# Sorting edges into cells: one-hot rows built column by column, weights turned first, smaller first batches

## The chip, the cores and the metric

One core of a Trainium2 chip runs the whole program. The metric is the device time of one execution in microseconds (us). The engines are TensorE (PE in the profile, its weight loads PEld), VectorE (DVE), ScalarE (ACT), GpSimd (POOL), and SyncE (SP), which only issues transfers and waits.

## The reference

Four graph layers follow each other on 1250 nodes with 512 features and 21250 edges (10000 pairs in both directions and a self loop for each node; `dst` is sorted in the input, but not cell by cell). Each layer normalises `x`, applies ReLU and adds its result to `x`.

- Layer 0: `x @ W_self.T + mean over neighbours(x) @ W_neigh.T + bias`, layer norm.
- Layer 1: two weighted graph convolutions with degree scaling, then a row norm.
- Layer 2: a message per edge from `h[src]` and 128 edge features through two linear layers, a sum per destination, a GRU cell, a batch norm with given statistics.
- Layer 3: a weighted neighbour sum and a linear layer.

Layers 0, 1 and 3 need `segment_sum` over the edges with three weightings: 1, `edge_weight`, `edge_weight1`. Layer 2 folds `W2` and `W_ih` into one matrix per gate (the products `m` and `c` below), which depends on weights only.

## The kernel before, in words

**Cells.** The 1250 nodes make NT = 10 tiles of 128. An edge belongs to one of 10 x 10 = 100 cells (tile of `dst`, tile of `src`). The kernel sorts the edges by cell into rows of the DRAM tensor `cell_rows`, each cell padded to whole chunks of 128, and later turns each chunk into a 128 x 128 block of three adjacency matrices by one product on PE.

**Where an edge goes.** Edges lie as 128 partitions x 168 columns (J = 168; only 167 are used, columns are grouped in 34 spans of SPAN = 5). DVE makes the one-hot rows `oh1` (columns x B1 = 101 cells, bf16) in four wide comparisons (L1506). PE counts with two products per span (`count_span`, L1146): `before` is the count of each cell in earlier spans of all partitions, row by row, and `total` the count over all. DVE turns these into `base_b`, the first place of each span in each cell, split into a high and a low byte (L1522 to L1539). PE then gives in `rank_spans` (L1155, L1158) for a slot of up to 5 spans the place of the first edge of a kind, from `sums1` (the sum of the five one-hots of a span, by DVE's `sum_spans`) and `row_of` (a selector of rows, L1509). DVE's `pick_spans` (L1560, L1568) multiplies that with the one-hots and sums; with `own`, the number of equal cells earlier in the same span (L1572 to L1575), this is the place of each edge. Seven short steps (L1583 to L1589) make the row index `idx1` of a batch of spans (`BATCHES` = 0, 2, 6, 14, 24, 34 in spans; `SUMMED` gives the slots) and release POOL by `order_ready[0]`.

**The cell scatter.** POOL waits for a batch, copies payload and indices of a span into one of two rings (`index_span`, L712 and L713), and issues one indirect DMA of 128 rows for each column (`scatter_span`, L720): 168 in all. When all have landed, SP loads `cell_rows` back (`cells_loaded`), and ACT, DVE, POOL and PE start to build blocks (L875, L1742, L772, L1213).

**What runs beside the scatter.** PE turns ten weight blocks (`turn_weights`, transposes, L1133), ACT copies them out of PSUM (L833) into one of two buffers `ws`, and SP loads raw weights (two buffers, L515) and stores the turned ones. For the three `ih` blocks PE also makes the products `m` and `c` (L1191) right behind each block. DVE sorts the edges once more by the tile of `dst` (`places`, with the product `prefix2` on PE), then SP loads `x`, and DVE, PE and ACT do the first normalisation and two linear products for each of ten tiles (`he`, `hsT`, `ys`, `zs`; PE L1123). SP also zeroes the DRAM tensors `cell_rows` (one transfer) and `dst_rows` (six of 2 MB), both ahead of the first raw weight in its queue.

**Order.** Each engine runs its own list in order; semaphores tie them. On PE the list was: counts of all spans, wait for `base_ready`, then slots and weight blocks in turn.

Of the kernel before, what the change touches and what calls it, by code (L numbers as in the profile page):

```python
# [29 lines left out]
BF16 = mybir.dt.bfloat16  # L30
# [4 lines left out]
P = 128  # L35
# [11 lines left out]
J = -(-(JV + 1) // COL) * COL  # L47
# [37 lines left out]
def build_gnn(nc, x_in, src_in, dst_in, attr_in, w_in, w1_in, w_self, w_neigh, b0, gamma0, beta0,  # L85
# [19 lines left out]
    with ExitStack() as ctx:  # L105
# [92 lines left out]
        ones_b = sort_part(P // 2, BF16)  # L198
        base_b = sort_part(B1 // 2 + 1, BF16)[:, 0:B1]
# [3 lines left out]
        assert scur[0] <= 2 * AW  # L203
# [14 lines left out]
        cell_b = temp(SPAN * SPANS // 2).bitcast(BF16)  # L218
        own, same = temp(SPAN * SPANS), temp(SPAN * SPANS)
# [101 lines left out]
        ering = sb("ering", [P, COL, EW])  # L321

# [14 lines left out]
        sums1_ready = sem("sums1_ready")  # L337
        weights_copied = sem("weights_copied")
# [71 lines left out]
        PREFIX2_AFTER = 7  # L410
        X_AFTER = 8
# [4 lines left out]
        for n, (name, third) in enumerate(blocks):  # L416
            act_jobs += [("w", n, k) for k in range(5 if n == 0 else KT)]
            if blocks[n - 1][0][0:2] == "ih":
                act_jobs += [("m", blocks[n - 1][1], k) for k in range(KT)] + [("c", blocks[n - 1][1])]
# [35 lines left out]
        wj = {b: A[("w", b, KT - 1 if b else 4)] + 1 for b in range(len(blocks))}  # L455
        raw_src = {"w1h": w1_2, "ih0": w_ih, "ih1": w_ih, "ih2": w_ih, "hh0": w_hh, "hh1": w_hh,
# [24 lines left out]
        def _(sp):  # L481
# [11 lines left out]
            sp.wait_ge(zero_ready, 1)  # L493
            zc = (CELL_CHUNKS + SPARE) * 4
            sp.dma_start(cell_rows.rearrange("(p c) w -> p (c w)", p=P), h.rearrange("p t d -> p (t d)")[:, 0:zc]).then_inc(cells_zeroed, 16)
            for k in range(KT):
                sp.dma_start(b2_col[:, k:k + 1], b2_2[k * P:(k + 1) * P].rearrange("(p a) -> p a", a=1)).then_inc(b2_loaded, 16)
            zd = (DST_CHUNKS + SPARE) * EW
            part = zd // 6
            dz = dst_rows.rearrange("(p c) w -> p (c w)", p=P)  # L500
            for k in range(6):
                sp.dma_start(dz[:, k * part:(k + 1) * part], h.rearrange("p t d -> p (t d)")[:, 0:part]).then_inc(zeroed, 16)

            for n, (name, third) in enumerate(blocks):
                if n == X_AFTER:
                    sp.wait_ge(sorted_all, 1)
                    sp.wait_ge(x_free, 1)
                    for t in range(NT):
                        m = P if t + 1 < NT else LAST
                        sp.dma_start(xs[0:m, t], x_in[t * P:t * P + m, :]).then_inc(xe_loaded[t], 16)  # L510
# [6 lines left out]
                if n == 3:  # L517
                    sp.wait_ge(zeroed, 16 * 6)
# [3 lines left out]
                if n == len(blocks) - 1:  # L522
                    sp.wait_ge(b2_ready, 1)
                    for k, v in enumerate((b0, gamma0, beta0)):
                        sp.dma_start(vec[:, k], v.rearrange("(a f) -> a f", a=1).to_broadcast([P, D])).then_inc(vec_loaded, 16)
                if blocks[n - 2][0][0:2] == "ih":
                    gate = blocks[n - 2][1]
                    sp.wait_ge(act_read, A[("c", gate)] + 1)
                    sp.dma_start(wt_dram[f"m{gate}"], m_out.rearrange("p k f -> p (k f)")).then_inc(m_stored, 16)
                    sp.dma_start(c_dram[gate], c_out).then_inc(m_stored, 16)  # L530
# [10 lines left out]
            sp.wait_ge(c_scattered[1], 16 * (J - SPAN * (SPANS // 2)))  # L541
# [3 lines left out]
            edge_v = attr_in[0:JV * P, :].rearrange("(p j) f -> p j f", j=JV)  # L545
            for q in range(2):
                sp.dma_start(ering[:, 4 * q:4 * q + 4, 0:DE], edge_v[:, 4 * q:4 * q + 4, :]).then_inc(e_loaded[q], 16)
# [124 lines left out]
        def _(pool):  # L672
# [23 lines left out]
            nc.gpsimd.memset(own, 0.0)  # L696
            nc.gpsimd.memset(base_b, 0.0)
            nc.gpsimd.memset(cell_b[:, J:], 0.0)
            nc.gpsimd.memset(oh1[:, J:].rearrange("p j b -> p (j b)"), 0.0).then_inc(const_ready, 1)
            nc.gpsimd.memset(ones[:], 1.0).then_inc(const_ready, 1)  # L700

            pool.wait_ge(cells_zeroed, 16)
# [22 lines left out]
            rest = J - SPAN * (SPANS - 1)  # L725
            for n in range(len(BATCHES) - 1):
# [15 lines left out]
            pool.wait_ge(zeroed, 16 * 6)  # L742
# [86 lines left out]
        def _(act):  # L829
# [9 lines left out]

            act.wait_ge(edges_loaded, 16 * 4)  # L840
# [3 lines left out]
            for n in range(len(blocks)):  # L844
                m = n - 2
                if 0 <= m < len(stored_blocks):
                    act.wait_ge(wt_stored[m % 2], 16 * (m // 2 + 1) + (16 if m % 2 == 0 else 0))
                elif m >= 0:
                    act.wait_ge(for_act, A[("c", blocks[m][1])] + 1)
                if blocks[n][0] == "self":  # L850
                    root(("he", 1), one_rstd[:])
                for k in range(KT):
                    copy_job(("w", n, k), ws[:, n % 2, k])
                if n == 0:
                    copy_job(("w", 0, 4), tiles[:, 0])
                if blocks[n][0] == "neigh":
                    root(("he", 0), one_rstd[:])
                if blocks[n - 1][0][0:2] == "ih":
                    gate = blocks[n - 1][1]
                    if gate:  # L860
                        act.wait_ge(m_stored, 32 * gate)
                    for k in range(KT):
                        copy_job(("m", gate, k), m_out[:, k])
                    copy_job(("c", gate), c_out)
# [231 lines left out]
        def _(pe):  # L1096
# [45 lines left out]
            def count_span(g):  # L1142

                n = columns(g) * B1
                for job, left in (("before", later[:, SPANS - 1 - g:SPANS - 1 - g + P]), ("total", ones_b)):
                    ins = nc.tensor.matmul(dve_bank(job)[:, 0:n], left, hot_span(g, columns(g)), start=g == 0, stop=g == SPANS - 1)  # L1146
                    if g == SPANS - 1:
                        ins.then_inc(for_dve, 1)
# [12 lines left out]

            pe.wait_ge(sort_const, 1)
# [4 lines left out]
            pe.wait_ge(const_ready, 8)  # L1167
            pe.wait_ge(base_ready, 1)
            for n in range(len(blocks)):
                if n < 2:  # L1170
                    rank_spans(n)
                elif n == 2:
                    rank_spans(2)
                    rank_spans(3)
                elif n < 5:
                    rank_spans(n + 1)
                turn_weights(n)
                if n == 6:
                    rank_spans(6)
                if blocks[n - 1][0][0:2] == "ih":  # L1180

                    gate = blocks[n - 1][1]
# [898 lines left out]
```

## Time and profile before

| | us |
|---|---|
| median of 3 runs (lowest 1367.62, highest 1372.83) | 1371.41 |
| the profiled execution | 1371.79 |
| its span in the trace | 1370.0 |
| first indirect DMA of the cell scatter starts | 43.85 |
| last one starts | 290.04 |
| cells are back, first GpSimd product of the block stage starts | 296.82 |

Shares of the span by engine: PE busy 87%, DVE 74%, POOL 51%, ACT 42%. These are averages over stages. From 44 to 296 us PE is busy 161.68 of 252 us, DVE 142.21 and POOL 179.85; from 296 us to the end PE is busy 1013.42 of 1074. So the first 296 us have to be read by their own waits. A DMA_INDIRECT row on POOL is the time in which GpSimd writes one indirect transfer. In a timeline the first column is the start, the second the duration, and the brackets give the idle time before and what ended it. Instructions of one engine overlap a little in such rows, so the cost of one in a run of many is the distance between starts, not the duration.

### The profile page before, as it was taken

The page shows a single profiled execution, that of the slowest core. Times are in us where ns is not written, and L with a number is a line of the kernel's source. Part 1 is how long each engine was busy: PE and PEld are TensorE (multiplying, and loading weights), DVE is VectorE, ACT ScalarE, POOL GpSimd, SP SyncE. Part 2 cuts the span into 40 slices and gives each one's busy share as a digit, 9 for nine tenths or more (in the row PEclk, how much of TensorE's full clock was granted, in tenths as well). Part 3 has the DMA queues.
Part 4 walks back from the last instruction along what each step waited for, and adds up shares of the span by engine and source line. Part 5 has one row for each costly group of instructions (what it writes and reads, how often), then busy time and mean ns, then how long its engine had stood idle before and what let it go on. Part 6 is the DMA issues. An engine that isn't in the chain of part 4 may idle for free.

```text
span 1370.0 us, 20255 instructions
## 1 busy us (share of the span) xinstructions
PE 1192.8 (87%) x4298; PEld 745.9 (54%) x4298; DVE 1016.8 (74%) x2113; ACT 572.2 (42%) x1461; POOL 700.4 (51%) x828
## 2 busy tenths in 40 slices
PE   5468499429999999999998899999999899998998
PEld 2343244214444445558876555454454588886787
DVE  9796845129999998642387688898888899888433
ACT  0221121027777730220011388787788833334211
POOL 0577777768888843776676366666666100000000
PEclk9679699859999999999999999999999999999999
DMA  8851512130000036333226677776777200002231
GB/s 331 313 197 40 199 63 79 55 113 18 27 20 25 12 146 223 112 114 131 82 88 181 204 224 221 223 234 207 226 213 221 58 1 0 1 0 89 77 96 37
DMA packets 87258, 167.89 MB, mean 123 GB/s; under 512 B 16124, under 2 KB 44670, under 8 KB 84644
## 3 DMA queue, kind: packets, MB, share of 16 engines
q1 hardware_dynamic: 59588, 102.69, 22.5%
q0 software_dynamic: 25472, 59.97, 14.4%
q10 hardware_dynamic: 2144, 4.59, 1.0%
q8 instruction: 25, 0.41, 0.1%
q14 instruction: 29, 0.24, 0.1%
HBM read 115.96 MB, written 51.23 MB: 122 GB/s over the span
## 4 chain that ended last, share of the span: by engine, by line
PE 62%; POOL 14%; issue 10%; DVE 8%; DVEq 2%; DMA 2%; ACT 1%; POOLq 0%; SPq 0%; ACTq 0%
PE pb L1348 11%; POOL cell_rows L720 10%; PE pb L1248 6%; PE pb L1240 6%; PE pb L1443 5%; PE pb L1213 5%; PE pb L1416 4%; PE pb L1418 4%; PE pb L1417 4%; PE pb L1362 3%; PE pb L1364 2%; PE pb L1365 2%; PE pb L1123 2%; PE pb L1341 2%; DMA p_rows<-tiles 2%
## 5 line engine op out<-in xcount | busy, mean ns | idle before, releaser
L765 POOL DMA_INDIRECT dst_rows<-ering,gidx x168 | 171.7, 1022 | 101.3 <-issue 95.4
L1348 PE MATMUL pb<-arena 128*128 128x512 f32 x368 | 191.2, 602 | 14.1 <-ACT arena L990 13.8
L720 POOL DMA_INDIRECT cell_rows<-tiles,gidx x168 | 166.8, 993 | 68.1 <-issue 47.4
L819 POOL DMA_INDIRECT arena<-p_rows,arena x96 | 100.5, 1047 | 78.6 <-issue 24.9
L1213 PE MATMUL pb<-arena 128*128 128x384 f32 x268 | 96.7, 504 | 42.4 <-POOL arena L772 42.2
L875 ACT ACTIVATE arena<-iota,free 128x128 f32<-128x128 f32 x266 | 92.3, 394 | 85.9 <-DMA free<-cell_rows 39.2
L1917 DVE TENSOR_TENSOR arena<-pb,arena 128x512 f32<-128x512 f32 x184 | 122.3, 683 | 5.7 <-DMA arena<-p_rows,arena 3.3
L1924 DVE SCALAR_TENSOR_TENSOR low<-arena,high 128x512 fp32r<-128x512 f32 x138 | 95.2, 690 | 31.4 <-ACT high L997 22.0
L819 POOL DMA_INDIRECT arena<-p_rows,ws x88 | 89.1, 1013 | 53.9 <-issue 29.0
L1213 PE MATMUL pb<-tiles,arena 128*128 128x384 f32 x264 | 94.4, 501 | 15.2 <-DVE arena L1761 9.4
L1759 DVE TENSOR_TENSOR arena<-pb,arena 128x192 f32 x266 | 94.1, 354 | 12.8 <-PE pb L1213 12.7
L1364 PE MATMUL pb<-high,low 128*128 128x512 f32 x138 | 99.5, 721 | 2.5 <-DVE arena L1932 2.0
L1213 PEld LDWEIGHTS pb<-arena 128*128 128x128 f32 x268 | 48.8, 193 | 85.2 <-ACT arena L880 43.4
L1417 PE MATMUL pb<-gru_low,high 128*128 128x512 f32 x240 | 93.5, 390 | 0.0
L1761 DVE TENSOR_TENSOR arena<-pb,arena 128x192 f32 x266 | 92.6, 348 | 0.1
L1123 PE MATMUL pb<-ws,tiles 128*128 128x512 f32 x200 | 89.2, 593 | 2.8 <-issue 1.6
L1240 PE MATMUL pb<-arena 128*128 128x256 f32 x400 | 88.2, 380 | 2.0 <-DVE arena L1856 1.4
L997 ACT ACTIVATE high<-arena 128x512 fp32r<-128x512 f32 x138 | 84.9, 615 | 7.2 <-DVE arena L1917 5.8
L1240 PEld LDWEIGHTS pb<-arena 128*128 128x128 f32 x400 | 75.8, 190 | 16.0 <-issue 4.3
L1213 PEld LDWEIGHTS pb<-tiles,arena 128*128 128x128 f32 x264 | 45.5, 189 | 63.9 <-ACT arena L880 34.0
L1348 PEld LDWEIGHTS pb<-arena 128*128 128x128 f32 x368 | 55.7, 191 | 45.0 <-ACT arena L990 19.7
L1443 PE MATMUL pb<-parts 128*128 128x512 f32 x300 | 74.1, 407 | 5.9 <-DVE parts L1980 4.2
(331 smaller groups left out, 2550.6 us busy)
## 6 DMA issues: line engine op xcount, KB each, us to landing
dst_rows<-arena SPq DMA_DIRECT2D x6, 2046.0 KB, 17.5
ering<-in_edge_attr_dram SPq DMA_DIRECT2D x41, 256.0 KB
arena<-adj SPq DMA_DIRECT2D x10, 640.0 KB, 4.1
arena<-dst_rows SPq DMA_DIRECT2D x24, 264.0 KB
arena<-wt_gru SPq DMA_DIRECT2D x48, 128.0 KB
ws<-dst_rows SPq DMA_DIRECT2D x22, 264.0 KB
arena<-in_x_dram SPq DMA_DIRECT2D x18, 256.0 KB, 7.8
arena<-in_L_gnn_W_hh_dram SPq DMA_DIRECT2D x3, 1024.0 KB
```

Of the source, the lines that this page charges most:

```text
L720: nc.gpsimd.indirect_dma_start(cell_rows[:, :], bass.IndirectOffsetOnAxis(gidx[:, SPAN * a + k:SPAN * a + k + 1], 0), cring[:, a, k], None ...
L765: nc.gpsimd.indirect_dma_start(dst_rows[:, :], bass.IndirectOffsetOnAxis(gidx[:, k:k + 1], 0), ering[:, k, :], None).then_inc(e_scattered[ ...
L819: nc.gpsimd.indirect_dma_start(rows[:, k % GROUP, :], None, p_rows[:, :], bass.IndirectOffsetOnAxis(edge_rows(k).bitcast(I32)[:, 0, DE:DE ...
L1123: ins = nc.tensor.matmul(b[:, 0:wide], x[:, k], w[:, k], start=m == 0, stop=m == n - 1)
L1213: nc.tensor.matmul(pb[k % 4][:, 0:3 * P], ohs[:, k], ohd(k, 1).rearrange("p a m d -> p (a m d)"), start=True, stop=True).then_inc(block_do ...
L1240: ins = nc.tensor.matmul(b[:, 0:wide], blocks_of[:, s], rows_of[:, s, 0:wide], start=s == 0, stop=s == NT - 1)
L1348: nc.tensor.matmul(e_bank(k)[:], erowT[:, k % 4], w1e_sb, start=True, stop=True).then_inc(edge_mm, 1)
L1364: nc.tensor.matmul(sums, hot, high[:, k % 4], start=k % 2 == 0, stop=False)
L1417: nc.tensor.matmul(bank[:], parts[0][:, k], low_w, start=False, stop=False)
L1443: ins = nc.tensor.matmul(b[:], a3[:, t % 2, left, k], h3[:, right, k], start=first and k == rows_of[0] and left + right == 0, stop=last an ...
L1917: vtt(row, e_bank(k)[:], row, ALU.add).then_inc(msg_added, 1)
L1924: vstt(low_part[:, k % 4], rows[:, k % GROUP], 0.0, high[:, k % 4].bitcast(F32), ALU.max, ALU.subtract).then_inc(msg_ready, 1)
```

## The change

- **One-hots per column.** `oh1` is made by 168 `tensor_scalar` instructions of 102 bf16 elements, each comparing a row of cell numbers with a per-partition scalar in SBUF (a pointer operand: `cell_f[:, j:j+1]`, now fp32). B1 is 102. There are five parts for PE (`O_PARTS`) instead of four.
- **One count product per span.** `total` is no longer counted by 34 products; DVE reduces `before`, and one fp32 product with `last_row` (a matrix whose row 127 is ones) copies its last row, where all counts stand, to every partition.
- **Moved off DVE.** `row_of` is made by ACT with two activations (Abs, then Relu of 1 minus it) over 128 x 4352; `own` is made by POOL (four subtractions, three additions) and ACT (Abs, Relu over 128 x 680). DVE's long zeroing of `h` is gone; one memset of the edge ring (128 x 1056) is the source of zeros.
- **Weights first.** The first raw weights are at the head of SP's queue after the edge columns; PE turns block 0 ahead of the counts. `cell_rows` is zeroed by two transfers behind the second raw weight, `dst_rows` by 24 smaller transfers behind the tenth. Turned `ih` blocks go to a place of their own (`ih_turned`), and all fifteen products `m` and `c` follow after the tenth block, with the last slot and `prefix2` between them. Loading `x` comes after their stores in SP's queue.
- **Small batches.** `BATCHES` = 0, 1, 2, 4, 8, 14, 24, 34 and ten slots instead of eight; the scatter leaves out the unused column 168, so it issues 167.

```diff
-        B1 = CELLS + 1
+        B1 = CELLS + 2
-        O_PARTS = [0, 9, 18, 27, SPANS]
-        BATCHES = [0, 2, 6, 14, 24, SPANS]
-        SUMMED = [0, 2, 6, 10, 14, 19, 24, 29, SPANS]
+        O_PARTS = [0, 9, 18, 26, 31, SPANS]
+        BATCHES = [0, 1, 2, 4, 8, 14, 24, SPANS]
+        SUMMED = [0, 1, 2, 4, 8, 11, 14, 19, 24, 29, SPANS]
...
+                if n == 1:
+                    sp.wait_ge(zero_ready, 1)
...
+                    for k in range(CELL_ZEROS):
+                        sp.dma_start(cz[:, k * cell_zeros:(k + 1) * cell_zeros], zeros[:, 0:cell_zeros]).then_inc(cells_zeroed, 16)
...
+            for k in range(DST_ZEROS):
+                sp.dma_start(dz[:, k * dst_zeros:(k + 1) * dst_zeros], zeros[:, 0:dst_zeros]).then_inc(zeroed, 16)
...
+            for gate in range(3):
+                sp.wait_ge(act_read, A[("c", gate)] + 1)
+                sp.dma_start(wt_dram[f"m{gate}"], m_out.rearrange("p k f -> p (k f)")).then_inc(m_stored, 16)
+                sp.dma_start(c_dram[gate], c_out).then_inc(m_stored, 16)
+            sp.wait_ge(sorted_all, 1)
+            sp.wait_ge(x_free, 1)
...
+            for d in range(1, SPAN):
+                nc.gpsimd.tensor_tensor(apart[:, d - 1, :, d:], cell5[:, :, d:], cell5[:, :, 0:SPAN - d],
+                                        ALU.subtract).then_inc(own_apart, 1)
...
-            rest = J - SPAN * (SPANS - 1)
+            rest = USED - SPAN * (SPANS - 1)
...
+            nc.scalar.activation(row_of, iob_f[:, 0:SPANS].unsqueeze(2).to_broadcast([P, SPANS, P]), ACT.Abs,
+                                 bias=row_p).then_inc(row_ready, 1)
...
-                for job, left in (("before", later[:, SPANS - 1 - g:SPANS - 1 - g + P]), ("total", ones_b)):
-                    ins = nc.tensor.matmul(dve_bank(job)[:, 0:n], left, hot_span(g, columns(g)), start=g == 0, stop=g == SPANS - 1)
...
+                ins = nc.tensor.matmul(dve_bank("before")[:, 0:n], later[:, SPANS - 1 - g:SPANS - 1 - g + P],
+                                       hot_span(g, columns(g)), start=g == 0, stop=g == SPANS - 1)
...
+            pe.wait_ge(const_ready, 9)
+            turn_weights(0)
             pe.wait_ge(sort_const, 1)
...
+            pe.wait_ge(counts_summed, 1)
+            nc.tensor.matmul(dve_bank("total")[:, 0:B1], last_row, before, start=True, stop=True).then_inc(for_dve, 1)
+            pe.wait_ge(base_ready, 2)
+            pe.wait_ge(row_ready, 2)
+            rank_spans(0)
+            turn_weights(1)
+            rank_spans(1)
...
-                vtt(oh1[:, c], iob[:, 0:B1].unsqueeze(1).to_broadcast([P, n, B1]),
-                    cell_b[:, c].unsqueeze(2).to_broadcast([P, n, B1]), ALU.is_equal).then_inc(hot1_ready, 1)
-
-            vts(row_of, iob_f[:, 0:SPANS].unsqueeze(2).to_broadcast([P, SPANS, P]), row_p, None, ALU.is_equal)
...
+                for j in range(SPAN * O_PARTS[q], min(SPAN * O_PARTS[q + 1], J)):
+                    ins = vts(oh1[:, j], iob[:, 0:B1], cell_f[:, j:j + 1], None, ALU.is_equal)
+                ins.then_inc(hot1_ready, 1)
...
+            sum_spans(0)
...
+            nc.vector.tensor_reduce(before, whole(dve_bank("before")), AX_X, ALU.add).then_inc(dve_read, 1)
+            dve.wait_ge(dve_read, V["before"] + 1)
+            dve.sem_inc(counts_summed, 1)
...
+            vts(cnti, dve_bank("total")[:, 0:B1], float(P - 1), None, ALU.add).then_inc(dve_read, 1)
...
             nc.vector.memset(xs[:, NT - 1], 0.0).then_inc(x_free, 1)
+            dve.wait_ge(for_act, A[("c", 2)] + 1)
```

## Rows read from the trace of the kernel before

**Rows 1.** The page: the chain that ended last, shares by line.
```profile
PE pb L1348 11%; POOL cell_rows L720 10%; PE pb L1248 6%; PE pb L1240 6%; PE pb L1443 5%; PE pb L1213 5%; PE pb L1416 4%; PE pb L1418 4%; PE pb L1417 4%; PE pb L1362 3%; PE pb L1364 2%; PE pb L1365 2%; PE pb L1123 2%; PE pb L1341 2%; DMA p_rows<-tiles 2%
```

**Rows 2.** The chain in order of time, first 297 us: start, duration, piece.
```profile
13.41 17.08 PE pb L1146 x67
43.85 1.34 POOL cell_rows L720
...
290.04 2.10 DMA cell_rows<-tiles,gidx
296.82 1.05 POOL arena L772
```

**Rows 3.** Timeline of POOL: the first scatters of two spans that follow each other.
```profile
66.47 0.98 POOL L720 DMA_INDIRECT cell_rows<-tiles,gidx  x1 [0.79 <-issue]
...
73.68 0.99 POOL L720 DMA_INDIRECT cell_rows<-tiles,gidx  x1 [0.81 <-issue]
```

**Rows 4.** Timeline of DVE from the cell numbers to the first indices.
```profile
7.02 0.24 DVE L1497 TENSOR_SCALAR arena<-arena 128x168 int32<-128x168 int32 x1
7.18 0.24 DVE L1498 TENSOR_SCALAR arena<-arena 128x168 int32<-128x168 int32 x1
...
8.37 18.04 DVE L1506 TENSOR_TENSOR arena<-arena 128x4545 bf16<-128x4545 bf16 x4
26.32 2.48 DVE L1509 TENSOR_SCALAR arena<-arena 128x4352 bf16<-128x4352 f32 x1
...
30.59 0.68 DVE L1522 TENSOR_REDUCE arena<-pb 128x101 f32<-128x505 f32 x1 [0.37 <-PE pb L1146]
...
31.90 0.21 DVE L1526 TENSOR_SCALAR arena<-arena 128x101 f32<-128x101 f32 x1
...
34.64 0.21 DVE L1538 CAST arena<-arena 34x101 bf16<-34x101 int32 x1
...
37.92 0.68 DVE L1560 TENSOR_TENSOR arena<-pb,arena 128x505 f32<-128x505 f32 x1
...
40.78 0.17 DVE L1583 TENSOR_TENSOR arena<-arena 128x10 int32<-128x10 f32 x1
...
42.02 0.17 DVE L1589 CAST idx<-arena 128x10 int32<-128x10 f32 x1
```

**Rows 5.** DVE instructions with a pointer operand: timeline, then one line's durations.
```profile
6.35 0.15 DVE L1490 CAST arena<-arena 128x104 bf16<-128x104 f32 x1
6.42 0.27 DVE L1491 TENSOR_SCALAR arena<-arena 128x128 bf16<-128x128 f32 x1
6.61 0.24 DVE L1492 TENSOR_SCALAR arena<-arena 128x162 bf16<-128x162 f32 x1
```
```profile
L1641 DVE SCALAR_TENSOR_TENSOR arena<-arena x11: 380/383/404, 133.1 to 136.2; 128x168 f32<-128x168 bf16 x11
```

**Rows 6.** Timelines of PE's weight loads and of PE, first 60 us.
```profile
18.43 0.15 PEld L1146 LDWEIGHTS pb<-arena 128*128 128x128 bf16 x1 [0.27 <-issue]
```
```profile
36.29 0.38 PE L1158 MATMUL pb<-arena 128*128 128x101 bf16 x2
45.22 4.47 PE L1133 MATMUL pb<-ident,arena 128*128 128x128 f32 x20 [8.55 <-DMA arena<-in_L_gnn_W_dram]
```

**Rows 7.** Windows: busy us (instructions) of each engine, TensorE clock, DMA share, GB/s.
```profile
0.00:25.00 25.00, 11.59 (x42) 4.78 (x43) 22.86 (x18) 2.08 (x3) 3.08 (x21) 1.00 0.74 294
```

**Rows 8.** Groups of ACT instructions by line and shape.
```profile
L1042 ACT CAST parts<-arena 128x1280 fp32r<-128x1280 f32 x10 | 12.6, 1262 | 5.1 <-PE pb L1443 5.1
```

**Rows 9.** Timeline of PE: products of one gate, last linear products before the cells.
```profile
112.85 17.33 PE L1191 MATMUL pb<-ws,arena 128*128 128x512 f32 x40
...
241.85 13.90 PE L1123 MATMUL pb<-ws,tiles 128*128 128x512 f32 x32
```

**Rows 10.** Timelines of SP (loading x) and DVE (first tile half normalised).
```profile
143.42 4.87 SPq L510 DMA_DIRECT2D arena<-in_x_dram  x10
```
```profile
168.47 0.50 DVE L1699 TENSOR_SCALAR arena<-arena 128x512 f32<-128x512 f32 x1
```

More of the change, by code:

```diff
@@ L46 @@
 COL = 8
-J = -(-(JV + 1) // COL) * COL
+USED = JV + 1
+J = -(-USED // COL) * COL
 PAIR = 2 * P
@@ L217, in build_gnn @@
         st_f, dt_f = temp(J), temp(J)
-        cell_b = temp(SPAN * SPANS // 2).bitcast(BF16)
-        own, same = temp(SPAN * SPANS), temp(SPAN * SPANS)
+        cell_f = temp(SPAN * SPANS)
+        own, own_rest = temp(SPAN * SPANS), temp(SPAN * SPANS)
+        apart = temp(4 * SPAN * SPANS).rearrange("p (d g j) -> p d g j", d=4, g=SPANS)
+        last_row = temp(P)
         row_p = temp(1)
@@ L844, in _ @@
             for n in range(len(blocks)):
-                m = n - 2
-                if 0 <= m < len(stored_blocks):
+                m = {2: 0, 3: 1, 4: 2, 8: 4, 9: 3}.get(n)
+                if m is not None:
                     act.wait_ge(wt_stored[m % 2], 16 * (m // 2 + 1) + (16 if m % 2 == 0 else 0))
[L848 to L851, printed above, removed]
                 for k in range(KT):
-                    copy_job(("w", n, k), ws[:, n % 2, k])
+                    copy_job(("w", n, k), turned_block(n)[:, k])
                 if n == 0:
                     copy_job(("w", 0, 4), tiles[:, 0])
[L856 to L864, printed above, removed]
+            for gate in range(3):
+                if gate:
+                    act.wait_ge(m_stored, 32 * gate)
+                for k in range(KT):
+                    copy_job(("m", gate, k), m_out[:, k])
+                copy_job(("c", gate), c_out)
+            root(("he", 0), one_rstd[:])
+            root(("he", 1), one_rstd[:])
             def flat(t4):
@@ L1166, in _ @@
                     count_span(g)
[L1167 to L1182, printed above, removed]
-                    pe.wait_ge(w2_loaded, 16)
-                    pe.wait_ge(b2_ready, 1)
-                    pe.wait_ge(act_read, wj[n - 1])
-                    for k in range(KT + 1):
-                        job = ("m", gate, k) if k < KT else ("c", gate)
-                        b = to_act(job)
-                        for o in range(KT):
-                            left = w2_raw[:, o, k * P:(k + 1) * P] if k < KT else b2_wide[:, o]
-                            ins = nc.tensor.matmul(b[:], left, ws[:, (n - 1) % 2, o], start=o == 0, stop=o == KT - 1)
-                        ins.then_inc(for_act, 1)
-                if n == 6:
-                    rank_spans(7)
-                if n == PREFIX2_AFTER:
-                    pe.wait_ge(totals_ready, 1)
-                    sort_products("prefix2", B2)
@@ new lines, in _, with fold @@
+            turn_weights(5)
+            rank_spans(6)
+            turn_weights(6)
+            turn_weights(7)
+            rank_spans(7)
+            turn_weights(8)
+            rank_spans(8)
+            turn_weights(9)
+            def fold(gate, products):
+                for k in products:
+                    job = ("m", gate, k) if k < KT else ("c", gate)
+                    b = to_act(job)
+                    for o in range(KT):
+                        left = w2_raw[:, o, k * P:(k + 1) * P] if k < KT else b2_wide[:, o]
+                        ins = nc.tensor.matmul(b[:], left, ih_turned[:, gate, o], start=o == 0, stop=o == KT - 1)
+                    ins.then_inc(for_act, 1)
@@ L1199, in _ @@
+            pe.wait_ge(w2_loaded, 16)
+            pe.wait_ge(b2_ready, 1)
+            pe.wait_ge(act_read, wj[7])
+            fold(0, range(0, 2))
+            rank_spans(9)
+            fold(0, range(2, 5))
+            fold(1, range(KT + 1))
+            fold(2, range(0, 2))
+            pe.wait_ge(totals_ready, 1)
+            sort_products("prefix2", B2)
+            fold(2, range(2, KT + 1))
             pe.wait_ge(sorted_all, 1)
```

190 lines of the change are left out of this document (102 added, 88 removed).

## The prediction

> **What bounds the kernel now.** I read the page's chain first. Most of it is PE after 296 us, but one item is not PE: the cell scatter on POOL holds 10% of the chain [rows 1]. The chain in order of time shows why [rows 2]: up to 30.5 us it is the counts on PE, which follow DVE's one-hots, then nothing long but scatters from 43.85 to 290.04 us, the landing, the load of the cells, and the first product of the block stage at 296.82. Only then does the rest of the kernel begin, and the diff leaves that rest alone. So the change can move the time in two ways only: by when the first scatter starts, and by how long the row of scatters takes. Everything else it moves lies beside the scatter and counts only if it ends later than the cells.
>
> The POOL timeline gives the pace: a span of five takes 73.68 - 66.47 = 7.21 us [rows 3]. The batches after the first hardly ever make it wait. The profiled execution took 1371.79 us, of which the span is 1370.0; the median of the runs is 1371.41, 0.4 less, and I take that 0.4 off at the end.
>
> **The path to the first scatter now** [rows 4]. Cell numbers from 7.02; one-hots from 8.37 to 26.41; row selector and small steps to 30.2; counts reduced from 30.59; base places 31.90 to about 35.1; span sums and own ranks until 37.92; two picks until 40.78; seven index steps until 42.19; 1.66 us later the scatter at 43.85 [rows 2]. Now the same path with the change, step by step.
>
> *Start.* DVE no longer clears h (3.4 us) ahead of the cell numbers, so the edge columns decide. They cannot be there before about 3.2 us (their issue) and were there at 7.02. I take 4.6. The numbers took 8.37 - 7.02 = 1.35 us and get one more semaphore: one-hots from 6.0 (bounds 4.7 to 8.4).
>
> *One-hots per column.* This is the price that decides. Two neighbours without a pointer operand, 168 elements, start 0.16 us apart [rows 4]. With reductions at 0.68 us for 505 elements and 0.17 for ten, an element costs about 1.03 ns, and a single-input step half of it: 0.16 is 0.087 of elements and 0.07 fixed. With a pointer operand the trace has two cases [rows 5]. The eleven of L1641 start 3.1/10 = 0.31 us apart (on finer reading 0.304) for 168 elements at 1.03 ns, 0.173: fixed 0.13. L1491 is followed 0.19 us later, with 128 elements at half price, 0.066: fixed 0.124. So a pointer costs some 0.055 us more for each instruction. I take 0.127 fixed and, for 102 narrow elements, 0.027, between nothing and the half price 0.053: 0.154 us a column, bounds 0.13 and 0.18. 168 x 0.154 = 25.9 us against 18.0 now. One-hots end at 31.9, 5.5 us later than now.
>
> The Trainium skill has a rule for this (VectorE: DVE Perf Modes, on the TRN2 errata, where SBUF sources pay a fixed extra latency per instruction): 58 cycles and the elements divided by the perf mode, which it gives as four for bf16 tensor_scalar. By it a column would cost (58 + 102/4)/0.96 = 87 ns, an estimate, and all 168 would take 14.6 us. The same section says that many small tiles pay the fixed cost each time and large ones once, which speaks against this edit. The rows without a pointer are near its 58 cycles; those with one are not.
>
> *Counts.* PE ran them at first one in 0.15 + 0.27 = 0.42 us [rows 6], later half of that. There are 34 now instead of 68, and weight block 0 ahead of them: 20 transposes, 4.47 us [rows 6], from about 12 us when its raw weights land (both loads, 2.3 MB at 294 GB/s [rows 7], take 7.9 us from about 5, the first of them less). Done at 16.5, before DVE is; so DVE bounds, and only the last part of three spans is left: 3 x 0.42 = 1.3. Counts end at 33.2. DVE hides this with the sums of slot 0 and the low bits of the ends.
>
> *Total.* Reduction 0.1 + 0.68; semaphore 0.1; the fp32 product 0.5 (bounds 0.2 and 1: a transpose costs 0.22, an fp32 product with 512 columns 0.43); then the chain from L1526 to L1538, 2.74 us now [rows 4], less two steps of 0.25, 2.25; two copies 0.45. Base places at 37.3. Now they were ready at 35.1.
>
> *First slot.* PE 0.6 (its last products for two spans ended at 36.67 [rows 6], 0.6 after the sums that released them); one pick instead of two, (40.78 - 37.92)/2 = 1.43 us; index steps 42.19 - 40.78 = 1.41; own ranks no longer on this path, saving 2.0 us where they stood. Indices ready at 40.7, first scatter 1.66 us later: **42.4**.
>
> So the wide steps taken off DVE (row selector 2.48 us, one reduction, own ranks, one pick, the clearing) pay for the slower one-hots and leave 43.85 - 42.4 = 1.4 us.
>
> *One scatter fewer.* The last spans keep the same pace as the first, five scatters in a span and 0.8 us between spans, (7.21 - 0.83)/5 = 1.28 us each, so 167 instead of 168 saves 1.28 us.
>
> **What costs nothing, and its cover.** ACT's row selector: 1280 elements take 1.262 us [rows 8], so about 3.9 us for 4352; twice that and the two short ones end near 13 us; it is wanted at 37. POOL's own ranks: seven short operations before 12 us, wanted at 39. The batches: after the first, POOL is busy 7.21 us a span, DVE needs 1.43 for a pick, 1.4 for indices and 1 to 1.4 for sums, so the second batch (5.2 us of DVE work) is in time, and so are the wider ones; on PE each slot stands behind weight blocks that need some 7 us each (two-buffer loading), at most two between slots, against batches of 14 us and more. Zeroing dst_rows (12.6 MB, 37 us of queue) moves from under the first weights to under the scatter, wanted at 290. Own place for the turned ih blocks: nothing.
>
> The longest move is behind it. The three folds (17.3 us each [rows 9]) now stand together after the tenth block, near 96 us; the first store of m waits in SP's queue behind the 12.6 MB of zeros, so ACT's second fold starts near 131, prefix2 near 144 instead of 130, and x is loaded near 157 instead of 143 [rows 10]. The first tile then is normalised near 183 instead of 169, and ten tiles at 7.3 us, PE's work up to the cells, end near 258. Now PE ends at 255.8 [rows 9], since it was held by the last fold until 181. The cells come at 294: a cover of some 35 us.
>
> **Sum.** 1371.8 - 1.4 - 1.3 = 1369.1; less 0.4 for the median: **1368.7 us**, 0.2% faster, which is no difference that can be told. I call that bound 0.5%, 6.9 us, about what this measurement can tell from no change. The likeliest case's own range: column price 0.13 to 0.18 gives -4.0 and +4.4, start and product -1.5 and +2.5: 1363 to 1375.
>
> **Rivals.**
>
> *A. The pointer is hidden, as if it were read under the instruction before.* A column then costs 0.07 + 0.027 = 0.097 us; one-hots end at 6.0 + 16.3 = 22.3 and PE bounds the counts: 16.5 + 13 x 0.42 + 21 x 0.21 = 26.4 (24.5 if the clock is already up after the weights). That is 6.8 us earlier than above; first scatter at 35.6, total 1361.9, faster. For it: L1491 starts only 0.07 us after the instruction before it, which has 104 elements [rows 5], so that both together are no dearer than two without pointer. Against it: the eleven of L1641. The Trainium skill's 87 ns (the section named above) would give the same, since PE bounds. It decides below 0.129 a column, where 1364.5 is reached.
>
> *B. The column instructions do not overlap at all.* A step whose result is awaited costs 0.15 + 0.05 for the pointer + 0.027 = 0.23 us and so would these, for example while POOL's additions and DVE want the same memory path. 168 x 0.23 = 38.6, first scatter 42.4 + 12.7 = 55.1, total 1381.4: slower. For it: 168 distinct outputs in close order are nowhere in the trace. Against: every unlinked pair overlaps by 0.08. It decides from 0.21 a column, where 1378.3 is reached.
>
> *C. The work beside the scatter overtakes it.* If folds, stores and zeros push the load of x past 190 us instead of 157, the ten tiles end after the cells and each further us is lost. At 203 us it costs some 10: 1378.7. For it: three waits in a row on the stores of m. Against: 35 us of cover.
>
> *D. The change does its first step and no more*: the first scatter comes earlier, but POOL then waits for slot 1 behind weight block 1. The order has rank_spans(0), block 1, rank_spans(1): 16 transposes, 3.6 us, against 6.4 us of scatters. Each us above that is lost; it would eat up A's gain only with a late second weight, landed by 15 us. It ends within 0.5%.
>
> **How the numbers follow.** Forecast and D together 0.53; A 0.33; B 0.08; C 0.04; 0.02 for the rest, on the slow side. So faster 0.34 (A and the edge of the forecast), same 0.53, slower 0.13. The range reaches over A's value with its faster clock and over the forecast's upper end: 1360 to 1376; B and C are left out, 0.12, and some edge of A.
>
> **What would show it.** In the profile after: distance of the column one-hots' starts (0.154; 0.10 in A; 0.23 in B); the end of the counts (33.2); the first scatter at 42.4 (A 35.6, B 55); last scatter 2.7 us earlier than 290.04; first block product near 294; no idle time of POOL between batches; PE's last linear product near 258; the stretch behind the cells, 1073.2 us, unchanged. The prediction is wrong if the column price is outside 0.13 to 0.18, or if the later stage changes its length.

## Result: 1.6% slower, and the loss is in a loop that the diff doesn't touch

The changed kernel took 1393.78 us (median of 4 runs, 1390.96 to 1399.89) against 1372.12 us before (4 runs, 1367.62 to 1373.95): ratio 1.0162, interval 1.0133 to 1.0191. The forecast was 1368.7, with a range of 1360 to 1376. The profiled execution took 1390.96 us.

Up to the block stage almost everything came as forecast. DVE's and PE's timelines of the changed kernel, answering to [rows 4, 6]:

```profile
4.44 0.25 DVE L1548 TENSOR_SCALAR arena<-arena 128x168 int32<-128x168 int32 x1 [1.59 <-DMA arena<-in_dst_dram]
...
5.99 27.60 DVE L1557 TENSOR_SCALAR arena<-arena 128x102 bf16<-128x102 bf16 x168 [0.25 <-DVE arena L1552]
...
35.14 0.69 DVE L1583 TENSOR_REDUCE arena<-pb 128x102 f32<-128x510 f32 x1 [0.34 <-PE pb L1185]
...
39.05 0.21 DVE L1600 CAST arena<-arena 34x102 bf16<-34x102 int32 x1
...
42.44 0.17 DVE L1635 CAST idx<-arena 128x5 int32<-128x5 f32 x1
```
```profile
10.96 4.42 PE L1173 MATMUL pb<-ident,arena 128*128 128x128 f32 x20 [10.96 <-DMA arena<-in_L_gnn_W_dram]
...
31.62 3.41 PE L1185 MATMUL pb<-arena 128*128 128x510 bf16 x8 [1.36 <-DVE arena L1557]
```

One-hots start at 5.99 and end at 33.59, counts end at 35.03, base places are there at 39.26. POOL's timeline and PE's around the cells [rows 2, 9] have the rest: first scatter 44.19, and the first block product at 296.49, 1.5 us earlier than the 298.00 of before.

```profile
44.19 1.19 POOL L750 DMA_INDIRECT cell_rows<-tiles,gidx  x1 [0.91 <-POOL gidx L743]
```
```profile
249.19 13.90 PE L1163 MATMUL pb<-ws,tiles 128*128 128x512 f32 x32
296.49 4.18 PE L1268 MATMUL pb<-arena 128*128 128x384 f32 x6 [33.40 <-POOL arena L807]
```

So the change stood 1.5 us ahead when the "unchanged" rest began. The windows of each kernel cut that rest in two: the block stage (first block product to the first product of the next stage), and all behind it. First before, then after; the columns are the engines' busy time, PE's granted clock, DMA share and GB/s.

```profile
296.80:500.00 203.20, 185.77 (x532) 94.39 (x532) 190.28 (x661) 146.20 (x396) 172.19 (x181) 0.99 0.09 31
500.00:1370.00 870.00, 827.65 (x3160) 554.36 (x3160) 643.29 (x1110) 377.54 (x972) 344.61 (x387) 0.99 0.43 134
```
```profile
295.30:521.90 226.60, 193.73 (x532) 102.01 (x532) 191.35 (x659) 146.24 (x396) 171.92 (x181) 0.93 0.09 29
521.90:1389.00 867.10, 825.33 (x3160) 552.78 (x3160) 642.83 (x1112) 377.30 (x972) 347.67 (x387) 0.99 0.43 134
```

The same 532 products take 24 us more: from product to product (298.00 to 500.54 us before, 296.49 to 523.12 after) the stage is 226.6 us long instead of 202.5 (+24.1). Behind it the kernel is 3.6 us shorter. Together: -1.5 + 24.1 - 3.6 = +19.0, the difference of the two spans.

Who waits in the block stage? The view of DVE's waits has a row in the changed kernel that the kernel before doesn't have: the front addition of the block loop (L1804; L1759 before) stands idle 18 times, 25.6 us in all, and nothing that the profile shows ends the wait.

```profile
DVE arena L1804 <- issue: 25.6, 18, 4.0
```

Its timeline puts the long ones 28 us apart, six of them, 3.68 to 4.02 us each. 28 us is one pass of DVE's block loop (32 chunks), and between two of them, in mid pass, stands a short one of 0.3 us:

```profile
351.51 0.36 DVE L1804 TENSOR_TENSOR arena<-pb,arena 128x192 f32 x1 [4.02 <-issue]
...
363.86 0.36 DVE L1804 TENSOR_TENSOR arena<-pb,arena 128x192 f32 x1 [0.29 <-issue]
...
379.44 0.36 DVE L1804 TENSOR_TENSOR arena<-pb,arena 128x192 f32 x1 [3.84 <-issue]
```

In the kernel before, the same place of the loop has 1.11 us (`PE pb L1213` ended it), and the middle none:

```profile
349.43 0.36 DVE L1759 TENSOR_TENSOR arena<-pb,arena 128x192 f32 x1 [1.11 <-PE pb L1213]
```

What arrives in these stretches is code. The DMA view has queue q14, kind "instruction", 8 KB a packet. In the window 330 to 500 us of the kernel before it moved 5 packets, in 330 to 523 us of the changed kernel 34. Before, then after:

```profile
q14 instruction: 5, 0.04, 0.1%
```
```profile
q14 instruction: 34, 0.28, 0.6%
```

**The theory.** DVE's program comes in pieces of 8 KB, which is 128 instructions of 64 bytes in the compiled program. The block loop has 284 instructions. The change puts 176 more instructions on DVE ahead of it (168 columns for 4 wide comparisons are nearly all of it), so the loop's first instruction moves from number 670 to 846, counted in the compiled programs. 284 instructions lie in three pieces or in four, by where the first of them stands. In four, each return to the loop's head finds its code gone, and it is read again: 37 pieces in the whole stage, against 7 before. **The rival**: the added work itself (DVE's instructions, the zeroing of dst_rows now under the scatter, POOL's or SP's new order) disturbs the stage.

The Trainium skill (Runtime: NRT & Kernel Launch, Instruction fetch mechanics) has the rule in general: a taken branch whose target isn't in the window of two blocks of 16 KiB stalls until it is fetched. That rule spoke against this change, and the prediction didn't weigh it. The packets here are of 8 KB, not 16, and two blocks of 256 instructions would hold this loop at number 846 as well as at 670, so by its sizes this change should have cost nothing here. The Trainium skill's total of 32 KiB would fit: it is four packets, three of the loop and one read ahead. That is an argument, and no row shows it. The runs below test the place.

### The profile page after: what moved, and what is told of

Read it like the earlier page. It is cut to its first block, busy times and chain, and to the rows that moved or that the text cites. A ratio compares the mean times of both kernels' runs of the same rounds, so it can differ in the third digit from the quotient of the medians.

```text
span 1389.0 us, 20391 instructions
## 1 busy us (share of the span) xinstructions
PE 1200.4 (86%) x4268; PEld 752.3 (54%) x4268; DVE 1022.2 (74%) x2286; ACT 580.9 (42%) x1465; POOL 704.9 (51%) x836
## 4 chain that ended last, share of the span: by engine, by line
PE 44%; POOL 19%; issue 18%; DVE 8%; DMA 6%; DVEq 3%; SPq 1%; POOLq 1%; ACT 1%; ACTq 0%
PE pb L1403 11%; POOL cell_rows L750 9%; POOL dst_rows L800 6%; PE pb L1498 5%; PE pb L1471 4%; PE pb L1268 4%; PE pb L1473 4%; PE pb L1472 4%; PE pb L1417 3%; PE pb L1419 2%; PE pb L1420 2%; DVE arena L1557 2%; PE pb L1396 2%; DVE arena L1806 2%; DMA ering<-in_edge_attr_dram 1%
## 5 line engine op out<-in xcount | busy, mean ns | idle before, releaser
L1268 PE MATMUL pb<-tiles,arena 128*128 128x384 f32 x264 | 104.4, 542 | 31.5 <-DVE arena L1806 28.2
L1804 DVE TENSOR_TENSOR arena<-pb,arena 128x192 f32 x266 | 94.0, 353 | 34.7 <-issue 25.6
L1268 PEld LDWEIGHTS pb<-tiles,arena 128*128 128x128 f32 x264 | 52.0, 208 | 82.3 <-issue 33.9
L1268 PEld LDWEIGHTS pb<-arena 128*128 128x128 f32 x268 | 50.1, 195 | 74.5 <-ACT arena L920 34.9
L872 ACT ACTIVATE one_rstd<-one_rstd 128x1 f32<-128x1 f32 x50 | 10.1, 203 | 182.7 <-DVE one_rstd L1720 98.9
L1295 PEld LDWEIGHTS pb<-arena 128*128 128x128 f32 x400 | 75.8, 190 | 16.0 <-issue 5.3
L807 POOL TENSOR_TENSOR tiles<-tiles,free 128x512 f32<-128x512 f32 x66 | 68.0, 1050 | 26.2 <-DVE tiles L1787 25.4
```

The source lines that it names most:

```text
L1268: nc.tensor.matmul(pb[k % 4][:, 0:3 * P], ohs[:, k], ohd(k, 1).rearrange("p a m d -> p (a m d)"), start=True, stop=True).then_inc(block_do ...
L1295: ins = nc.tensor.matmul(b[:, 0:wide], blocks_of[:, s], rows_of[:, s, 0:wide], start=s == 0, stop=s == NT - 1)
L1804: vtt(front, sums[:, :, 0:HALF], front, ALU.add).then_inc(front_added, 1)
```

## The experiments

They ran on two other chips, each ratio against runs of the kernel before on the same chip: runs 1, 2, 3 (48 added) and 6 where it took 1355.11 us, the others where it took 1354.53. (The difference to 1372 lies behind the block stage: 850 us there for 869.) The totals expected of runs 1, 2, 3 and 6 were worked out from the first chip's 1372 us, so their differences and stages are to be compared, not the totals. None of them leaves out or changes what is computed; the eighth adds work whose results nobody reads.

**1 and 2. The changed kernel, its loop moved by 8 and by 32 instructions.** The added instructions do nothing but count on a semaphore of their own.

```diff
             link(nc.vector.tensor_copy(counting, iota1[:]))
+            for _ in range(8):        # 32 in the second
+                dve.sem_inc(pad, 1)
```

> The changed kernel with 8 more DVE instructions (semaphore increments that nothing waits for) in DVE's idle time, just ahead of the block loop. Theory 1 (code loading): DVE's block loop has 284 instructions; the profile after shows five 8 KB code loads (128 instructions each) in every turn, where the kernel before shows none once the loop runs. Its last instructions have slid into a fourth such piece, and with the next piece that is loaded ahead, five do not stay resident. 8 more keep it there: stall of about 4 us at each of the loop's returns, block stage near 227 us, total 1391 to 1396. Theory 2 (the table loads at the head of each turn, or traffic, have become slower, not the place of the code): also 1391 to 1396. A control: the padding alone costs nothing.

> The same with 32 instead of 8, which pushes the start of the loop over a 128-instruction border, so that it lies in three pieces. Theory 1: no stall at the returns, block stage 203 us, total 1391 - 24 = 1367 (1364 to 1371), about the kernel before less the 1.6 us that its first products come earlier. Theory 2: no difference from 8, 1391 to 1396.

8 more: ratio 1.0173 (1.0131 to 1.0214), stage 227.3 us, six long idle times of 3.5 to 3.7 us. 32 more: **0.9961 (0.9948 to 0.9974)**, stage 202.25 us. The DMA view again, 8 more (330 to 523 us), then 32 more (330 to 495 us), and of the latter the window of the stage:

```profile
q14 instruction: 34, 0.28, 0.5%
```
```profile
q14 instruction: 4, 0.03, 0.1%
```
```profile
295.07:497.32 202.25, 185.22 (x532) 94.55 (x532) 191.03 (x662) 145.08 (x393) 170.91 (x180) 0.99 0.09 29
```

All of the change's work is in this kernel, and the loss is gone. The rival falls.

**3 and 4. The kernel before, its loop moved by 48 and by 80.** Number 718 stands as 846 does to a border (both 78 past a multiple of 128), 750 as 878.

```diff
             link(nc.vector.tensor_copy(counting, iota1[:]))
+            for _ in range(48):       # 80 in the other
+                dve.sem_inc(pad, 1)
```

> The kernel before, with nothing of the change, and 48 such instructions ahead of the loop, so that it starts at the same place within 128 as in the changed kernel (it adds 176, which is 128 + 48). Theory 1: the stall appears, total 1372 + 24 = 1396 (1392 to 1400). Theory 2: 1372, since nothing of the change is in it.

> The kernel before with 80 empty DVE instructions (semaphore increments) just ahead of its block loop, where 48 cost 1.8%. Code loading by position: the loop begins at DVE instruction 750, and with the code ahead of it its 284 instructions lie in four pieces of 128, at most, with none read again; no row of four idle microseconds at the loop's returns, some 6 fetches in the block stage, stage 202.5 us, ratio 0.998 to 1.002. Rival, that instructions ahead of the loop cost by their number or by the time they take: 80 should cost more than 48 did, ratio 1.02 or above.

48 more: **1.018 (1.0155 to 1.0204)**, stage 227.4 us, 37 pieces of code read in it, six long idle times of 3.7 to 3.9 us. 80 more: 1.0001 (0.9985 to 1.0017), stage 202.3 us, 6 pieces. Nothing but empty instructions makes the old kernel as slow as the new one, and more of them make it fast again. The waits of DVE with 48:

```profile
DVE arena L1760 <- issue: 26.1, 19, 3.9
```

**5. The changed kernel with a shorter loop.**

```diff
-PLACED = 4 * TURN
+PLACED = 2 * TURN
```

> The changed kernel with 16 chunks in each pass of DVE's block loop in place of 32: the loop is 142 instructions long and is run through twice as often. Code loading: a loop of that length is never longer than three pieces, so no return stalls, the stage takes about 203 us and the ratio is that of the changed kernel with 32 empty instructions, 0.996 (0.993 to 0.999). Rival, that the stall belongs to the return itself (a register, the table load): twice as many returns, twice as many stalls, some 45 us, ratio 1.035.

The loop's start moves as well, to number 714, which is 74 past a border.

1.0002 (0.9989 to 1.0016). No long idle time and 5 pieces of code in the stage, as the theory says; but the time missed its range. The stage took 206.8 us, not 203: every return costs DVE about 0.8 us of idle time, and there are more than twice as many.

```profile
322.99 0.36 DVE L1804 TENSOR_TENSOR arena<-pb,arena 128x192 f32 x1 [0.87 <-PE pb L1268]
```

In the loop of 32 chunks six ordinary returns cost 1.05 to 1.1 us each, put down to PE. I hadn't priced a return.

**6. Wide comparisons in place of the 168 columns.** It tries both halves of the story: fewer instructions ahead of the loop (number 684), and the column's price.

```diff
+        cell_b = temp(SPAN * SPANS // 2).bitcast(BF16)
...
+            link(nc.vector.tensor_copy(cell_b[:, 0:J], cell_f[:, 0:J]))
...
-                for j in range(SPAN * O_PARTS[q], min(SPAN * O_PARTS[q + 1], J)):
-                    ins = vts(oh1[:, j], iob[:, 0:B1], cell_f[:, j:j + 1], None, ALU.is_equal)
-                ins.then_inc(hot1_ready, 1)
+                c = slice(SPAN * O_PARTS[q], min(SPAN * O_PARTS[q + 1], J))
+                n = c.stop - c.start
+                vtt(oh1[:, c], iob[:, 0:B1].unsqueeze(1).to_broadcast([P, n, B1]),
+                    cell_b[:, c].unsqueeze(2).to_broadcast([P, n, B1]), ALU.is_equal).then_inc(hot1_ready, 1)
```

> The changed kernel with the four wide one-hot comparisons of before in place of the 168 column instructions (five parts). One-hots 18 us instead of 27.6, so first scatter near 34.8 instead of 44.2; the loop then starts 162 instructions earlier, in three pieces. Theory 1: 1391 - 24 - 9 = 1358 (1355 to 1363). Theory 2: 1391 - 9 = 1382.

0.9994 (0.9979 to 1.001): no stall (stage 202.6 us), but the first scatter came at 46.56, not 34.8, and later than with the columns (43.91 in the second run, on the same chip). I was wrong on this one. The timeline over all engines shows a chain across four of them:

```profile
5.88 14.89 POOL L724 TENSOR_TENSOR arena<-arena 128x136 f32<-128x136 f32 x4 [0.91 <-DVEq L1554]
6.28 18.89 DVE L1560 TENSOR_TENSOR arena<-arena 128x4590 bf16<-128x4590 bf16 x5
...
20.80 0.77 ACT L881 ACTIVATE arena<-arena 128x680 f32<-128x680 f32 x1 [13.99 <-POOL arena L724]
...
27.27 1.12 PE L1174 MATMUL pb<-ident,arena 128*128 128x128 f32 x4 [12.50 <-ACT ws L869]
...
28.18 9.31 PE L1186 MATMUL pb<-arena 128*128 128x510 bf16 x34
```

POOL's four subtractions for the own ranks, 1.20 us together in the changed kernel, take 14.89 us while DVE's wide comparisons run. One by one, three of the four end just behind a comparison: at 11.43, 16.39 and 20.77 us, where comparisons end at 11.22, 16.23 and 20.65. ACT waits for them, and behind ACT's wait stand its copies of weight block 0 out of PSUM; PE waits for those, and behind PE's wait stand the counts. The columns cost DVE 8.7 us more (27.60 against 18.89) and leave POOL room; the wide form pays it back at another place.

**7. The same, with ACT's order changed**: the copies of block 0 first, then the own ranks' steps and the two copies into pay1. PE's counts no longer stand behind POOL.

```diff
-            act.wait_ge(own_apart, SPAN - 1)
-            apart_flat = apart.rearrange("p d g j -> p (d g j)")
-            nc.scalar.activation(apart_flat, apart_flat, ACT.Abs).then_inc(own_equal, 1)
...
             for n in range(len(blocks)):
...
                 if n == 0:
                     copy_job(("w", 0, 4), tiles[:, 0])
+                    act.wait_ge(own_apart, SPAN - 1)
+                    apart_flat = apart.rearrange("p d g j -> p (d g j)")
+                    nc.scalar.activation(apart_flat, apart_flat, ACT.Abs).then_inc(own_equal, 1)
...
```

> The changed kernel with five wide bf16 comparisons in place of the 168 columns, and on ScalarE the copies of weight block 0 out of PSUM ahead of the own ranks' steps, so that TensorE's counts don't stand behind them. DVE's comparisons end at 25.1 us as in the run without the new order, the counts near 26.5 in place of 37.5, the base places near 31, the first scatter at 35.5 (34.5 to 37), last scatter 8 us earlier than in the changed kernel; DVE's loop begins at instruction 684, so no stall. Time against the kernel before: 9.5 to 12 us less, ratio 0.992 (0.990 to 0.994). Rival, that GpSimd's own ranks, held up by the wide comparisons until 21 us, set the end: own ranks then come after 30 us and the first scatter at 40 or later, ratio 0.996.

**0.9908 (0.9891 to 0.9925), 1343.35 us against 1354.53: faster than both kernels.** DVE's comparisons are as long as in the sixth run, POOL's subtractions too; only who stands behind them changed. PE's timeline and POOL's:

```profile
11.14 4.50 PE L1174 MATMUL pb<-ident,arena 128*128 128x128 f32 x20 [11.14 <-DMA arena<-in_L_gnn_W_dram]
15.44 4.79 PE L1186 MATMUL pb<-arena 128*128 128x510 bf16 x18
...
25.09 0.74 PE L1186 MATMUL pb<-arena 128*128 128x510 bf16 x3 [0.48 <-DVE arena L1560]
```
```profile
35.73 1.19 POOL L751 DMA_INDIRECT cell_rows<-tiles,gidx  x1 [0.91 <-POOL gidx L744]
```

Counts end at 25.8, and the first scatter is 8.2 us earlier than in the second run (43.91). Of the gain of some 11 us this is the largest part. The 5.3 us by which the second run was already ahead do not add to it in full: together they would be 13.5, and the block stage is 1.4 us longer here than there; what is left wasn't found.

**8. The price of a column by itself.** 111 comparisons more while DVE waits for the cells.

```diff
+            narrow_in = he[:, 3].bitcast(BF16)[:, 0:B1]
+            link(nc.vector.memset(narrow_in, 1.0))
+            narrow_out = he.rearrange("p t d -> p (t d)").bitcast(BF16)
+            for pointer, elements in ((True, B1), (False, B1), (True, 10), (False, 10)):
+                for k in range(24):
+                    number = ye[:, 1, k:k + 1] if pointer else 3.0
+                    ins = vts(narrow_out[:, B1 * k:B1 * k + elements], narrow_in[:, 0:elements], number, None, ALU.is_equal)
+                link(ins)
+            for k in range(15):
+                ins = vts(he[:, k // 5, B1 * (k % 5):B1 * (k % 5) + B1], ye[:, 0, 0:B1], ye[:, 1, k:k + 1], None, ALU.is_equal)
+            link(ins)
```

> The changed kernel with 111 comparisons more on DVE while it is idle ahead of the cells, in five rows: 24 of 102 bf16 elements with a pointer operand, 24 with a constant, 24 of 10 elements with a pointer, 24 with a constant, and 15 of 102 fp32 elements with a pointer. My working of the column's price (a pointer costs 0.055 us in each instruction, fixed part 0.127, 102 narrow elements 0.027 to 0.053): starts 0.16 us apart, then 0.11, 0.13, 0.08, and 0.23 for fp32. Rival A's reading, that the pointer is hidden: the first two rows are equal. Another, that the price came from GpSimd's side work at the same time: the first row is now below 0.15. As a by-product the loop starts at instruction 958, where code loading says no stall at its returns.

```profile
264.91 4.13 DVE L1789 TENSOR_SCALAR arena<-arena 128x102 bf16<-128x102 bf16 x24
...
269.07 2.61 DVE L1789 TENSOR_SCALAR arena<-arena 128x102 bf16<-128x102 bf16 x24
...
271.72 3.43 DVE L1789 TENSOR_SCALAR arena<-arena 128x10 bf16<-128x10 bf16 x24
```
```profile
277.51 2.88 DVE L1792 TENSOR_SCALAR arena<-arena 128x102 f32<-128x102 f32 x15
```

The first two rows have one shape and differ in the pointer alone. From start to start (the medians; the rows' durations hold a first and a last one that are longer) an instruction takes 0.156 us with a pointer and 0.096 without; with 10 elements 0.133 and 0.072; fp32 with a pointer 0.183. So a pointer costs 0.060 to 0.061 us each time and is not hidden, which ends rival A. 92 narrow elements cost 0.023 to 0.024 us, 0.26 ns each, a quarter of the 1.03 ns that the prediction read for fp32. The fp32 row missed what I had expected, 0.23: its 102 elements cost 0.053 over the fixed 0.130, which is the prediction's half price and not the full one. The Trainium skill's four elements a cycle for bf16 tensor_scalar (VectorE: DVE Perf Modes) is 0.26 ns at its 0.96 GHz, and the runs agree. Its 58 cycles, 0.060 us at that clock, are somewhat short of the 0.069 that is fixed without a pointer, and the pointer comes on top.

In the changed kernel itself a column took 27.60/168 = 0.164 on average. The 0.008 above these 0.156 is not the price of every column: its trace has 167 distances between starts, and 160 of them are 0.155 to 0.159. Only seven are longer, 0.21 to 0.45 us. They lie where POOL computes the own ranks, and are 1.27 us more together. Windows of L1557 in the changed kernel, then POOL's timeline:

```profile
5.99:7.04 1.05, 1.05 (x4) 1.00 0.74 195
10.22:33.60 23.38, 23.37 (x150) 0.82 0.50 166
```
```profile
5.88 1.20 POOL L723 TENSOR_TENSOR arena<-arena 128x136 f32<-128x136 f32 x4 [0.91 <-DVEq L1553]
8.77 0.48 POOL L727 TENSOR_TENSOR arena<-arena 128x170 f32<-128x170 f32 x1 [1.68 <-ACT arena L882]
```

That POOL's steps hold these seven up is read from the same times, and no run took them away. It is rival B's condition, true for seven columns out of 168.

As a by-product this kernel tests the loop's place once more. Its single time was 1351.97 us and its stage 202.6 us: no stall either, with the loop at number 958.

**All ten programs in one table.** The loop has 284 instructions in each but the short one.

```
kernel                  loop starts at   past a border of 128   code pieces in stage   stage us
before                  670              30                     7                      202.5
changed                 846              78                     37                     226.6
changed, 8 more         854              86                     37                     227.3
changed, 32 more        878              110                    6                      202.3
before, 48 more         718              78                     37                     227.4
before, 80 more         750              110                    6                      202.3
wide / wide and ACT     684              44                     7 / 7                  202.6 / 203.6
changed, price rows     958              62                     7                      202.6
changed, short loop     714              74                     5                      206.8
```

284 instructions need a fourth piece where they start over 100 past a border (128 x 3 - 284 = 100). The traces don't show at which address the program begins; if 23 to 38 instructions that the compiled program doesn't count lie ahead of it, all rows with the long loop fall into place: 78 and 86 need four pieces, 30, 44, 62 and 110 (with the offset, past the next border) don't. That the pieces end where I put them is inferred from this pattern; that place and not work decides, and that 37 pieces are read where it costs and 7 or fewer where it doesn't, is shown.

## Why the prediction was wrong

**The step that failed** is in the first paragraph: "the diff leaves that rest alone", and in the last list "the stretch behind the cells, 1073.2 us, unchanged". The source of the rest is the same and its place in DVE's program isn't. I counted an instruction's time and never its room. Of the 24.1 us, the six returns take 6 x (3.8 - 1.05) = 16.5. The twelve short waits that nothing released, five of 0.3 us in mid pass and seven of 0.2 just ahead of a return, take 25.6 - 22.8 = 2.8. The remaining 5 go with PE, which is busy 193.7 us instead of 185.8 for the same 532 products, at a granted clock of 0.93 instead of 0.99 (the window rows above). The trace shows where: behind each of the six pauses the granted clock falls from 2.4 to 1.2 GHz and then rises again. Eight products just ahead of a pause and eight just behind it, then windows around the fall:

```profile
455.74 2.82 PE L1268 MATMUL pb<-tiles,arena 128*128 128x384 f32 x8 [0.59 <-DVE arena L1806]
...
464.71 4.71 PE L1268 MATMUL pb<-tiles,arena 128*128 128x384 f32 x8 [3.57 <-DVE arena L1806]
```
```profile
459.00:464.70 5.70, 2.14 (x7) 1.00 0.05 16
465.80:469.00 3.20, 3.20 (x6) 0.50 0.00 0
469.20:473.00 3.80, 3.80 (x13) 1.00 0.05 18
```

The runs agree: the stage's clock is 0.93 in the three kernels that pause (the changed one, 8 more, 48 more) and 0.98 or 0.99 in the seven that don't. In the kernel before it stays at 2.4 GHz through the returns (1.00 from 345 to 489 us). The range of 1360 to 1376 and the 0.13 for slower had no term for any of this; none of the rivals was it, although the last list did name a later stage of changed length as a sign of being wrong. C, the nearest in kind, didn't happen: x was loaded at 159.7 (forecast 157), the last linear product ended at 263.1 (forecast 258), with 33 us of PE idle before the cells.

**The other steps.**
- *Start* 6.0: 5.99.
- *Column price* 0.154 (0.13 to 0.18): 0.164, so one-hots ended at 33.6 instead of 31.9. The parts were 0.130 fixed with pointer (I took 0.127) and 0.027 for 102 elements (I took 0.027); what is missing, 1.3 of the 1.7 us, is the seven columns beside POOL's arithmetic; the rest of the columns take 0.156.
- *Counts* 1.3 us behind the one-hots: 1.44. *Total and base places* 4.1 us more: 4.2. *First slot* 3.4 and 1.66: 3.35 and 1.6 (39.26 to 42.61 to 44.19).
- *First scatter* 42.4: 44.19. The whole miss is the end of the one-hots, 1.7.
- *One scatter fewer* and the start together 2.7: 1.5 in the first products on this chip, as the first scatter came 0.3 later than before instead of 1.4 earlier.
- *What costs nothing*: no batch made POOL wait; the row selector, own ranks, weights and zeros stayed hidden. The row selector on ACT ended at 12.4 (forecast 13), POOL's ranks at 10.3 (12).
- *The change without its accident* is the second run: 0.9961, by this ratio 5.3 us less (3.5 to 7.0), where the prediction's sum has 2.7. That is within the 0.5% that the forecast called no difference. Its first block product is 2.6 us earlier than that of the third run, which is the kernel before on the same chip; where the rest of the 5.3 lies wasn't found.

## What to carry to other kernels

A loop's cost can change when code is added ahead of it, on the same engine, anywhere in the program. When a diff turns few wide instructions into many small ones, count them, and look at each loop behind them. If the pieces end as inferred above, a body of 258 to 384 instructions lies in three or in four by where it starts; only 284 and 142 were run here, and 142 had no stall but paid its return more often. In a profile, look for idle time that nothing released, at one place of a loop, and for a grown count on the instruction queue. Empty instructions ahead of the loop tell whether it is this, if they are enough to carry it over a border: 32 did here, and 8 did not. And where an engine works in order, first place what others wait for: with the wide comparisons, moving one wait behind five copies took the ratio from 0.9994 to 0.9908, and the whole change without its accident had 0.9961.

## What the runs showed of the hardware

- Code of DVE comes in 8 KB packets. By its start, a loop of 284 instructions either reads next to nothing again (5 packets in 170 us) or 34 packets in 193 us, and then stands 3.5 to 4.0 us at each return, in place of 1.05. The starts that stall are 78 and 86 past a multiple of 128, those that don't 30, 44, 62 and 110.
- TensorE's granted clock fell from 2.4 to 1.2 GHz behind each of these pauses (3.57 us of idle time in the rows above): eight products took 4.71 us there for 2.82.
- A pointer operand costs DVE 0.060 us in each instruction, also back to back: 0.156 against 0.096 us for 102 bf16 elements, and 0.133 against 0.072 for 10.
- POOL's four fp32 subtractions of 34 to 136 elements took 14.89 us beside DVE's wide bf16 comparisons, three of them ending 0.1 to 0.2 us behind a comparison, and 1.20 us beside narrow ones with a pointer. Seven of the narrow ones took 0.21 to 0.45 us beside POOL's steps, for 0.156 elsewhere.
